# Cross attentions of a decoder: where VectorE's last norm scales and three of GpSimd's steps stand among the slots

## The reference

```python
q = split(norm(x) @ Wq + bq); k = split(ctx @ Wk + bk); v = split(ctx @ Wv + bv)
score = einsum('bhqd,bhkd->bhqk', q, k) / sqrt(8)
attn = einsum('bhqk,bhkd->bhqd', softmax(score), v)
x = x + (merge(attn) @ Wo + bo)
```

## Time and profile before

| | |
|---|---|
| median of 3 runs | 1825.69 us (1820.52 to 1826.11) |
| the profiled execution | 1817.44 us, of it 1815.4 us span |
| PE, DVE, ACT, POOL busy | 1389.0, 1237.3, 921.7, 337.8 us |
| layer 0's cross attention | from 237 to about 395 us |
| layer 1's cross attention | from about 654 to 834 us |
| layer 3's cross attention | from about 1613 to 1770 us |

### The profile page before, as it was taken

How to read it: one execution, slowest core, us unless ns; L and a number is a source line. 1 busy time by engine, 2 the same in 40 slices (tenths; PEclk the granted TensorE clock), 3 DMA queues, 4 the chain that set the end, 5 groups by cost and what they waited for, 6 DMA issues and landing times. The chain is left out here.

```text
span 1815.4 us, 31936 instructions
## 1 busy us (share of the span) xinstructions
PE 1389.0 (77%) x10666; PEld 859.8 (47%) x10666; DVE 1237.3 (68%) x4823; ACT 921.7 (51%) x2002; POOL 337.8 (19%) x360
## 2 busy tenths in 40 slices
PE   5897978871874668994455799999983995778884
PEld 2454434441763434442234456666653883544442
DVE  7888368875337868887666676777764224757887
ACT  4654357651322346655612587777751442136756
POOL 3320012111524135400021000000002333302200
PEclk9999999985997879996577899999995997679996
DMA  3220014211561013210010000000003672003300
GB/s 127 56 53 2 0 18 60 36 36 44 159 145 35 12 53 58 50 19 20 1 60 1 12 7 13 7 7 7 1 7 106 185 205 63 24 18 52 51 6 23
DMA packets 59361, 83.42 MB, mean 46 GB/s; under 512 B 8064, under 2 KB 46208, under 8 KB 58688
## 3 DMA queue, kind: packets, MB, share of 16 engines
q1 hardware_dynamic: 54208, 71.15, 15.8%
q0 software_dynamic: 4992, 10.23, 2.9%
HBM read 51.18 MB, written 9.18 MB: 33 GB/s over the span
## 5 line engine op out<-in xcount | busy, mean ns | idle before, releaser
L876 ACT ACTIVATE L_xattn_probs<-ps 128x1024 f32<-128x1024 f32 x192 | 196.7, 1024 | 82.0 <-PE ps L1069 77.2
L717 DVE TENSOR_REDUCE maxs<-ps 128x4 f32<-128x1024 f32 x128 | 156.4, 1222 | 30.8 <-PE ps L1045 30.3
L3504 ACT ACTIVATE wide_pr<-wide_sc,wide_nm 128x256 f32<-128x256 f32 x256 | 127.0, 497 | 13.2 <-DVE wide_nm L3432 12.7
L1580 POOL DMA_INDIRECT moe_xs<-normed,moe_table x92 | 87.1, 947 | 155.1 <-PE ps L1610 72.8
L1045 PE MATMUL ps<-keys,L_xattn_qs 64*128 64x256 bf16 x768 | 75.6, 275 | 45.4 <-DVE maxs L717 25.7
L1085 PE MATMUL ps<-L_xattn_probs,values 128*32 128x256 f32 x1536 | 103.2, 386 | 0.0
L711 DVE CUSTOM_DVE_ANT_0 L_xattn_masked_scores<-ps,L_xattn_maskQ 128x256 bf16<-128x256 f32 x256 | 93.1, 420 | 13.8 <-PE ps L1045 13.5
L3427 DVE COPY wide_prT<-ps 128x512 f32<-128x512 f32 x64 | 44.3, 692 | 84.5 <-PE ps L3545 84.4
L3402 DVE CUSTOM_DVE_ANT_0 wide_sc<-ps,wide_mask 128x256 f32<-128x256 f32 x256 | 93.2, 420 | 3.2 <-PE ps L3530 2.1
L2009 DVE SCALAR_TENSOR_TENSOR moe_z_sb<-ps,moe_wt,moe_a_sb 128x256 f32<-128x256 f32 x46 | 22.3, 484 | 93.2 <-ACT moe_a_sb L2040 93.2
L711 DVE CUSTOM_DVE_ANT_0 L_attn_masked_scores<-ps,L_attn_maskQ 128x128 bf16<-128x128 f32 (+1 forms) x256 | 76.0, 353 | 7.6 <-PE ps L1045 7.2
(11 more groups left out here) (629 smaller groups left out, 3642.0 us busy)
## 6 DMA issues: line engine op xcount, KB each, us to landing
moe_wt<-in_packed_experts SPq DMA_DIRECT2D x23, 707.0 KB, 4.3
moe_wt<-in_packed_experts SPq DMA_DIRECT2D x23, 384.0 KB, 3.4
keys<-L_xattn_k_parts SPq DMA_DIRECT2D x108, 64.0 KB
L_xattn_qs<-L_xattn_q_parts SPq DMA_DIRECT2D x108, 64.0 KB
expert_out<-moe_y SPq DMA_DIRECT2D x46, 128.0 KB, 1.8
weights<-in_packed_L_xattn SPq DMA_DIRECT2D x2, 1316.0 KB, 7.2
keys<-L_attn_k_parts SPq DMA_DIRECT2D x36, 64.0 KB
L_attn_qs<-L_attn_q_parts SPq DMA_DIRECT2D x36, 64.0 KB
```

Of the source, the lines that this page charges most:

```text
L717: v.tensor_reduce(nm, ps[:, BANK_M:BANK_M + 2, :].rearrange("p j (t n) -> p j t n", t=2), AX.X, ALU.max, negate=True).then_inc(S("m_used"), 1)
L876: a.activation(probs[:, s % RING, :, :, :].rearrange("p j t n -> p j (t n)"), ps[:, BANK_P:BANK_P + 2, :], ACT.Exp, scale=HD ** -0.5)\
L1580: g.indirect_dma_start(self.xs[:, j % BUFS, h * P:(h + 1) * P], None, C.normed, bass.IndirectOffsetOnAxis(self.table[:, n:n + 1], 0))\
L3504: ins = a.activation(pr[:, s % 3, j, qt, :], sc[:, s % 2, j, qt, :], ACT.Exp, bias=nm[:, s % 2, n:n + 1], accum_out=sums[:, s % 2, n:n + 1])
```

## The change

Three things move, and nothing is added or removed.

- In the unmasked layers 0 and 3 the 20 steps of the norm scales no longer go four to a place from place 0, but two to a place at the odd places from 5 on. They end at place 23. The drain at place 12 is left out there.
- In all three cross attentions GpSimd's split of pair 1's keys moves from places 3, 4, 5 to places 4, 5, 6.
- In all three GpSimd's bias on x moves from place 3 of each window to place 14.

```diff
-                    stages = [(remainder, 3, 12, 1), (second, 4, 13, 1), (third, 5, 14, 1),
+                    stages = [(remainder, 4, 12, 1), (second, 5, 13, 1), (third, 6, 14, 1),
                               (remainder, 7, 22, 0), (second, 8, 23, 0), (third, 9, 24, 0)]
...
-                        m = p.job(3, 0)
+                        m = p.job(14, 0)
...
+                def some(side, put_off=False):
+                    if not put_off:
+                        next(side, None)
...
+                    calm = not masked and s < SLOTS
...
-                    if s == (4 if boundary is not None else 0):
+                    if s == (0 if rope else 4):
                         side = norms(2 * PT if rope else AHEAD, TILES)
...
-                    next(side, None)
+                    some(side, calm)
                     if 0 <= s - 1 < SLOTS:
                         add_max(s - 1)
...
-                    next(side, None)
+                    some(side, calm)
+                    if calm and s % 2:
+                        some(side)
+                        some(side)
...
-                    next(side, None)
+                    some(side, calm)
                     if g is not None:
                         normalise(g, inverted)
-                    next(side, None)
+                    some(side, calm)
...
-                    if p.t == 12 or boundary is not None and p.t == 3 and s < SLOTS:
+                    if p.t == 12 and (masked or s > WINDOW) or boundary is not None and p.t == 3 and s < SLOTS:
                         drain(side)
```

## The result

The changed kernel takes 1834.50 us in the median of its runs (1826.13 to 1839.02), the kernel before beside it on the same chip 1825.64 (1818.08 to 1833.38): a ratio of 1.0046, 95% interval 1.0033 to 1.0058. That is slower by 8.9 us (6.0 to 10.6), where 7.0 were forecast. The two layers don't share it as forecast. In the rows of the kernel after, the lines of the code from L836 on have moved by 8: `max_scores` is L1053, `prob_scores` L1077, VectorE's split L844.

A forecast was written before the change was run, and what follows sets the result against it. It took the end of GpSimd's third of pair 1's keys, which starts 24 DMAs, to bound slot 16 in layers 0 and 3. Layer 0 +4.2, layer 3 +2.8, layer 1 0: 1825.69 + 7.0 = 1832.7 us, range 1824.0 to 1837.0.

The forecast's parts named there:

- The stream: Pair 1's 24 key and query DMAs run without a gap; slot 16 opens 24.6 us after GpSimd's third of the keys.
- the keys' term: Layers 0 and 3: keys' split a place later opens slot 16 2.4 us later each, bounds 1.7 and 3.1.
- the 0.65 us that the opening should give back: Without four statistics in slot 0, first shifted scores come about 0.65 us earlier, between 0 and 0.86.
- The clock behind slot 16: TensorE's granted clock drops after longer idleness: layer 0 +1.4 us, bounds 0 and 2.8; layer 3 0.
- layer 3 has its drop already: 0: After slot 16 in layer 3 the clock already falls, so no added cost: 0, bounds -1.4 and +1.4.
- the clock stays low longer: Rival: both layers idle over 5 us at slot 16 and each loses another 1.4: 1835.5 us, chance 0.15.
- The norm steps: Leaving slots 0 to 4: about 0.65 us earlier; at places 5 and 7: 0.43 each; at 17 to 23: 0.
- The ring of the opening: TensorE's shifted scores, ScalarE's exponential and query copy wait on each other, 2.84 us a slot; norm steps in its shadow.
- the rival in which VectorE bounds the opening: Removing some 5.3 us of steps from slots 0 to 4 brings the third 2.3 us earlier: 1821.9 us, chance 0.13.
- all of slots 1 to 5 shifts by this and no more: Opening: moving the norm steps out shifts these slots only by the estimated 0.65 us.
- The bias: At place 30 it delays VectorE's split: 0.4 us a layer, bounds 0 and 0.6; elsewhere 0.
- Layer 1: Third 1.2 us later, but about 2 us of cover at slot 16: 0, bounds -0.3 and +0.8.

The follow-up runs named there:

- the keys alone: Kernel before with only pair 1's keys split at places 4, 5, 6 instead of 3, 4, 5: 1834.34 us, ratio 1.0018.
- the second measurement of the changed kernel: The whole change run once more against the kernel before: 1829.55 us, ratio 1.0035.
- the steps alone: Kernel before with only the 20 norm steps moved to odd places from 5 on: 1818.84 us, ratio 0.9977.
- the keys all at place 3: Kernel before with all three steps of pair 1's keys split at place 3: 1826.95 us, ratio 0.9983.
- The fillers: Changed kernel plus 22 matmuls of 512 columns while TensorE waits at slot 16, layers 0 and 3: 1834.71 us, ratio 1.0035 to the kernel before.
- the keys as before: Changed kernel with pair 1's keys back at places 3, 4, 5: 1824.02 us, ratio 0.9970; once more 1818.67 us, 0.9974, to the kernel before.
- the bias alone: Kernel before with only GpSimd's bias moved from place 3 to 14: 1823.25 us, ratio 1.0002.
- the queries later: Kernel before with pair 1's queries split at places 8, 9, 10 instead of 7, 8, 9: 1829.70 us, ratio 0.9997.

## Why the prediction was right, and where it was not

**The stream: right.** The steps of the argument held one by one in layer 0: the third waits for the split of slot 5 and starts 0.31 behind it (266.96 and 267.27), the share of the DMA engines has no gap, slot 16 opens 24.54 us behind the third. A line of experiments supports it: the third's place alone moves slot 16 (the keys alone), the queries' place doesn't. The idle time at slot 16 grew less than the 5.6 and 4.9 us of the forecast, to 5.13 and 3.78, and in the second measurement of the changed kernel to 5.08 and 4.80.

**The size of the keys' term: right.** Its two halves are read within each trace. The first is the 0.65 us that the opening should give back. Times from the start of the layer don't show it, because the clock is low there for another length in each trace. A row close ahead does: TensorE's projection of the context (L1160, L1168 after) and the first shifted scores, layer 0 before, then layer 0 after.

```profile
252.45 1.03 PE L1160 MATMUL ps<-ctxT,weights 128*128 128x256 f32 x4
...
254.79 0.40 PE L1069 MATMUL ps<-L_xattn_qm,keys 64*128 64x256 bf16 x4
```

```profile
252.56 1.03 PE L1168 MATMUL ps<-ctxT,weights 128*128 128x256 f32 x4
...
254.16 0.39 PE L1077 MATMUL ps<-L_xattn_qm,keys 64*128 64x256 bf16 x4
```

It is 2.34 us before and 1.60 after, and in layer 3 2.34 and 1.61: 0.74 was given back where 0.65 was forecast. The second half is read from the first shifted scores: the third ends 12.75 us behind them in layer 3, where it was 9.74, so 3.0 later, and the forecast had 2.4 + 0.65 = 3.05. Together that is 2.3 us a layer, for 2.4.

**The start of the layer: a term that the forecast didn't have.** In layer 0 the granted clock is 0.50 for the first 3 us of the layer before and for the first 9 after; the projection comes 15.46 and 16.24 us behind the first weight DMA, 0.8 later. In layer 3 it is the other way round, as the first stretch before and after shows, and the projection comes at 16.39 and 14.82, 1.6 earlier:

```profile
1612.00:1622.00 10.00, 8.12 (x20) 4.41 (x21) 0.80 (x2) 5.00 (x11) 2.92 (x3) 0.50 0.29 81
```

```profile
1631.60:1641.60 10.00, 8.14 (x31) 4.36 (x32) 2.50 (x4) 7.20 (x14) 2.92 (x3) 0.85 0.29 81
```

Both lengths occur with the norm steps in place and with them moved: some nine microseconds in 6 of 10 such starts and in 9 of 12, three in the others. Layer 0's start lies ahead of all that the change moves, though it is long in all six traces with the steps moved and in two of the other five. I take it as no work of the change; no run shows what decides it.

So layer 3, forecast at +2.8, shows +0.15: of its 2.3 at slot 16 the start took back 1.6, and the shorter distance from third to slot 16 (23.20 for 23.90) the other 0.7. In the second measurement of the changed kernel layer 3 is 4.0 us longer than in the kernel before (164.03), and layer 0 4.8 (162.87).

**A term that was missing: a low clock inside the opening.** In layer 0 slot 16 is 4.5 us later, not 2.4: of it 2.3 are the forecast's term and 0.8 the start of the layer. Shifted scores of slots 3 and 4, layer 0 of the kernel after, and the same in layer 3:

```profile
262.69 0.61 PE L1077 MATMUL ps<-L_xattn_qm,keys 64*128 64x256 bf16 x4 [0.61 <-ACT L_xattn_probs L884]
267.49 0.38 PE L1077 MATMUL ps<-L_xattn_qm,keys 64*128 64x256 bf16 x4
...
1656.54 0.40 PE L1077 MATMUL ps<-L_xattn_qm,keys 64*128 64x256 bf16 x4 [0.61 <-ACT L_xattn_probs L884]
1659.82 0.38 PE L1077 MATMUL ps<-L_xattn_qm,keys 64*128 64x256 bf16 x4
```

The same slot takes 4.80 us at the low clock and 3.28 at the full one: 1.5 us, and 2.3 + 0.8 + 1.5 are the 4.5, to a tenth. This low stretch isn't a fixed part of the change. In the traces with the norm steps moved, it stands in 8 of 12 openings of layers 0 and 3 (in layer 0 only for the changed kernel, in layer 3 only in its second measurement, in both with the steps alone); with the steps in place it stands in none of 8, and in both with the keys all at place 3. How the layer begins goes with it: with the steps moved it stands in 8 of the 9 openings whose layer starts with some nine microseconds at the low clock, and in none of the 3 that start with three; but with the steps in place 4 of the 8 start with nine, and none has it. So both the moved steps and the start of the layer seem to have to do with it; no run here isolates either, and the cause stays open. If the moved steps do bring it, they bring it at a net gain, since the kernel with the steps alone is the faster one.

**The clock behind slot 16: right in kind, wrong in size.** Layer 0 was forecast to drop as layer 3 had: 1.4, measured 1.23. The step that failed is "layer 3 has its drop already: 0": the low stretch there is longer than before (0.62 in the mean from 1684 to 1691, where the earlier trace rows had 0.76 from 1665 to 1672), and it costs 0.53 more. The fillers show that both are the price of the wait. The rival "the clock stays low longer" put another 1.4 a layer on this. In this trace it has 0.53 in layer 3 and nothing in layer 0; in the second measurement slots 16 to 18 take 5.90 us in layer 0 and 5.48 in layer 3, so again one layer has some 0.5 of it.

**The norm steps: the mechanism was right, the sign of the remainder wrong.** The ring of the opening keeps its pace, as forecast: from the first to the sixth shifted scores it is 14.64 us in the kernel before, with the keys alone, and in layer 3 of the kernel after, with and without the 20 steps. So the rival in which VectorE bounds the opening is refuted as it was put: its -2.3 us at the third would need shorter slots. (The 5.3 us in it are also added up too low: 0.86, two of 1.0 and 14 of 0.2 are 5.7.) But it had a true core. The ring leaves VectorE's split of slot 4 free to come earlier within its slot, and the stream starts from a split, not from the ring. With the steps alone the third comes 1.1 us earlier and the kernel is 0.9977. The forecast's phrase "all of slots 1 to 5 shifts by this and no more" is the step that failed. For the changed kernel it did no harm to the sum, since it waits for the split of slot 5, where the two statistics of place 5 were forecast at 0.43 and measured at 0.40. But it hid what the later place of the keys costs once the steps are gone: 12.75 - 8.65 = 4.1 us at the third, with the steps moved, against 2.6 with the steps in place.

**The bias: 0.4 forecast at place 30, 0.1 measured.** The maxima of slots 30 and 32 in layer 0 of the kernel before; then the kernel after, with GpSimd's third, its bias, VectorE's split of slot 30 and the maxima of slots 30, 31 and 32.

```profile
318.30 1.23 DVE L717 TENSOR_REDUCE maxs<-ps 128x4 f32<-128x1024 f32 x1 [0.21 <-PE ps L1045]
...
322.09 1.23 DVE L717 TENSOR_REDUCE maxs<-ps 128x4 f32<-128x1024 f32 x1 [0.51 <-PE ps L1045]
```

```profile
323.51 1.16 POOL L546 TENSOR_TENSOR L_xattn_k_parts<-L_xattn_rest,L_xattn_k_parts 128x512 bf16<-128x512 f32 x1 [1.42 <-DVE maxs L844]
323.58 1.23 DVE L717 TENSOR_REDUCE maxs<-ps 128x4 f32<-128x1024 f32 x1 [0.22 <-PE ps L1053]
324.62 1.09 POOL L612 TENSOR_TENSOR x<-x,weights 128x512 f32<-128x512 f32 x1
325.29 0.46 DVE L844 TENSOR_TENSOR maxs<-maxs 128x4 bf16<-128x4 f32 x1
325.66 1.21 DVE L717 TENSOR_REDUCE maxs<-ps 128x4 f32<-128x1024 f32 x1
...
327.46 1.23 DVE L717 TENSOR_REDUCE maxs<-ps 128x4 f32<-128x1024 f32 x1 [0.31 <-PE ps L1053]
```

The split does wait: it takes 0.46 us for 0.17, 0.3 more, where over 0.5 was forecast. Most of that fell into idle time: VectorE waits 0.31 for TensorE at the maximum of slot 32 and waited 0.51 before, and from the maximum of slot 30 to that of slot 32 it is 3.88 us, for 3.79 before. So 0.1 a layer is left, in layer 3 as well. And the place where the bias did cost something, place 3 of the kernel before, was forecast at 0.

**Layer 1: covered, as forecast.** Its third ends 2.8 us later from the layer's start; 0.8 of it is there at the first shifted scores, about 1.0 is a longer low stretch of the clock, and the remaining 1.0 is the forecast's 1.2. Stretches ahead of slot 16, which opens at 723.77, against the earlier trace rows:

```profile
720.00:722.00 2.00, 1.85 (x24) 1.01 (x22) 1.97 (x13) 1.59 (x3) 1.67 (x2) 1.00 0.31 62
722.00:724.00 2.00, 2.00 (x28) 0.97 (x28) 1.53 (x10) 1.12 (x2) 0.00 (x0) 1.00 0.00 0
```

A share of 0.31 is about half a stretch at the level of 0.57, so the DMAs end near 721.1. The quiet ahead of the slot is 2.7 us, and with the 1.5 us taken off that pass in layer 0 between the last transfer (291.5) and the matmul (292.97), some 1.2 us of cover are left. TensorE doesn't wait, and the layer's 2.2 us are none of the keys' doing (in the second measurement it is 178.7 us long, shorter than before); slot 16 itself is 1.8 later, as the first shifted scores (0.8) and the low stretch (1.0) have it.

**The total.** The medians give +8.9 (6.0 to 10.6) where +7.0 was forecast, and the second measurement +5.8 (2.6 to 10.2); 7.0 lies within both. That the sum is this near is partly luck. The keys' term held (2.3 for 2.4, twice), the bias was put 0.3 too high in each of two layers, and the clock had 1.5 us in an opening and 0.5 behind slot 16 that weren't forecast. In the profiled execution the three cross attentions give 5.7 + 2.2 + 0.15 = 8.1, but layer 1's part comes from no wait, and those of layers 0 and 3 have the starts of the layers in them, +0.8 and -1.6. The difference to the kernel with the keys as before, 10.9 us, is what the later place costs once the steps are moved. The trace of the changed kernel and the first one with the keys as before, which have the same openings, give it as well: per layer 4.7 (56.65 - 51.95) and 3.85 (52.38 - 48.53) at slot 16, and behind it 1.2 and 1.9 of clock against 4.04, together 11.7.

## What to carry to other kernels

When a consumer waits for a train of transfers without a gap, look for what starts the train: here a delay of its first member went through to the end, and a delay of later members cost nothing as long as it opened no gap. A ring that sets the pace of a loop doesn't make the work in its shadow free: something that leaves the ring halfway, as the split that starts GpSimd and the DMAs does, is delayed by each small operation ahead of it. Of a change with several parts, run each alone before judging the whole: here the part that the forecast put at a gain of some 0.2 us a layer gained 4.9 us (0.5 to 8.0) alone, and one line, once that part was in, lost some 11.

## What the runs showed of the hardware that was not expected

- The granted clock can fall to half inside the opening, where TensorE works in each slot and waits 0.61 us at the shifted scores; it does so in some traces of one kernel and not in others. Layer 0 of the kernel after, the stretch right ahead of the low one (granted clock 1.00, TensorE busy 5.56 of 8.50 us):

```profile
254.00:262.50 8.50, 5.56 (x47) 2.46 (x43) 5.22 (x12) 5.86 (x9) 1.76 (x2) 1.00 0.00 1
```

  A low stretch of this kind cost 1.5 us on a loop of 2.84 us a slot, a longer one about 3 (17.88 - 14.64 over five slots, with the keys all at place 3).
- About an idle time of 1.86 to 2.57 us the clock fell in layer 3 and stayed at 1.00 in layer 0, in each of three traces (the kernel before, the bias alone, the queries later). About one of 3.78 to 5.25 it fell in all six cases of three traces. Filled with matmuls of 512 columns it didn't fall in either layer.
- Twelve transfers between parts of SBUF to 8 partitions each run for some 12.5 us at a share of 0.57 of the DMA engines (the share adds up packets that overlap: in the first 18 us of the kernel before it reads up to 1.11), and 24 for 24.6 from the operation that starts them to the matmul that waits, in every trace in which TensorE waited for them and the share had no gap (24.2 to 24.8, with 23.2 and 23.9 in layer 3 of the kernels after and before).
